# Graph layer on one core: pair products of a message tile in one run, then all its sums, with VectorE's other work behind the pairs

## The reference, cut to what matters

```python
def _L0_gnn_ref(h, V, w_comp, loop_w, bias, ffn_w, ffn_b, ln_g, ln_b, norm, src, dst, etype):
    Hb = jnp.einsum('ni,bio->bno', h, V)
    coef = w_comp[etype]
    m = coef[:, 0][:, None] * Hb[0][src]
    for b in range(1, nb):
        m = m + coef[:, b][:, None] * Hb[b][src]
    m = m * norm[:, None]
    agg = jax.ops.segment_sum(m, dst, num_segments=n_nodes)
    hn = jax.nn.relu(agg + h @ loop_w + bias)
    y = hn @ ffn_w.T + ffn_b + h
    mu = jnp.mean(y, axis=-1, keepdims=True)
    var = jnp.var(y, axis=-1, keepdims=True)
    return (y - mu) / jnp.sqrt(var + EPS) * ln_g + ln_b

x = _layernorm(x + _L0_gnn_ref(x, ..., edge_weight, src, dst, edge_type_8), axis=-1)
x = _layernorm(x + _L1_gnn_ref(x, edge_index, ...), axis=-1)   # two transformer_conv layers
```

## Time and profile before

| | us |
|---|---|
| median of 3 runs | 1980.98 (1979.08 to 1981.27) |
| the profiled execution | 1991.4 |
| its span, first to last instruction | 1989.5 |
| TensorE busy | 1911.6 (96%) |
| VectorE busy | 1450.3 (73%) |
| ScalarE busy | 1282.1 (64%) |
| GpSimd busy | 670.9 (34%) |

### The profile page before, as it was taken

The page is one execution under the profiler, slowest core; times in us unless marked ns, Lnnn a source line. Parts: engine busy times, 40 slices in busy tenths (PEclk is TensorE's granted clock), DMA queues, the critical chain, the costliest instruction groups (busy, mean ns, idle before and its releaser), DMA issues. The chain is left out here.

```text
span 1989.5 us, 53432 instructions
## 1 busy us (share of the span) xinstructions
PE 1911.6 (96%) x19165; PEld 1655.2 (83%) x19165; DVE 1450.3 (73%) x4127; ACT 1282.1 (64%) x2289; POOL 670.9 (34%) x802
## 2 busy tenths in 40 slices
PE   1799999999999999999998999999999999999998
PEld 1789999999999999999995788888887788888887
DVE  3888777878787878787852876666764777777775
ACT  1566767677767766776674666666666566666665
POOL 2576567656765666566500000000000000000000
PEclk9899999999999999999998999999999999999999
DMA  3011111111111111111112222222211332222320
GB/s 82 10 39 54 66 41 40 54 65 40 40 54 65 40 40 53 66 40 41 48 59 100 98 98 97 97 97 97 97 64 46 120 106 96 88 100 99 104 104 11
DMA packets 43018, 137.00 MB, mean 69 GB/s; under 512 B 9190, under 2 KB 24359, under 8 KB 36484
## 3 DMA queue, kind: packets, MB, share of 16 engines
q1 hardware_dynamic: 38484, 128.24, 18.0%
q0 software_dynamic: 4400, 6.80, 1.5%
HBM read 91.83 MB, written 43.20 MB: 68 GB/s over the span
## 5 line engine op out<-in xcount | busy, mean ns | idle before, releaser
L854 PE MATMUL ps<-matrixT,x_rows 125*128 125x256 f32 (+1 forms) x2500 | 563.5, 377 | 0.1
L854 PEld LDWEIGHTS ps<-matrixT,x_rows 125*128 125x128 f32 x2500 | 461.3, 190 | 48.4 <-issue 0.2
L945 ACT COPY matrixT<-ps 125x500 f32<-125x500 f32 (+2 forms) x800 | 382.7, 654 | 54.5 <-PE ps L842 54.1
L1710 DVE CUSTOM_DVE_ANT_0 scores_l<-ps,bias_rows_l 125x500 f32<-125x500 f32 (+1 forms) x700 | 390.0, 619 | 25.7 <-issue 24.9
L842 PE MATMUL ps<-high_weights,low_onehot 64*125 64x125 f32 x6300 | 377.6, 276 | 12.5 <-DVE high_weights L722 11.1
L842 PEld LDWEIGHTS ps<-high_weights,low_onehot 64*125 64x125 f32 x6300 | 362.2, 189 | 31.2 <-issue 17.9
L1611 ACT ACTIVATE scores_l<-scores_l,neg_max_l 125x1500 f32<-125x1500 f32 x200 | 317.3, 1600 | 7.3 <-DVE neg_max_l L1731 7.3
L1499 PEld LDWEIGHTS ps<-weightsT_l,values_l 125*64 125x64 f32 x5000 | 267.9, 136 | 36.4 <-issue 34.1
L1540 PE MATMUL ps<-eye,scores_l 125*125 125x125 f32 x2500 | 295.2, 275 | 0.0
L1540 PEld LDWEIGHTS ps<-eye,scores_l 125*125 125x125 f32 x2500 | 281.2, 189 | 10.1 <-issue 9.6
L1522 PE MATMUL ps<-kT_l,q_tile_l 64*125 64x500 f32 (+1 forms) x1400 | 286.9, 547 | 1.7 <-issue 1.6
(11 more groups left out here) (152 smaller groups left out, 1604.6 us busy)
## 6 DMA issues: line engine op xcount, KB each, us to landing
bias_rows_l<-bias SPq DMA_DIRECT2D x50, 1562.5 KB, 6.6
bias<-bias SPq DMA_DIRECT2D x75, 500.0 KB
x_rows<-in_x SPq DMA_DIRECT2D x1, 1562.5 KB
bias<-bias SPq DMA_DIRECT2D x25, 62.5 KB
x<-x_rows SPq DMA_DIRECT2D x25, 62.5 KB
x_rows_l<-x SPq DMA_DIRECT2D x25, 62.5 KB
out<-rows_l SPq DMA_DIRECT2D x25, 62.5 KB
dst_int<-in_dst SPq DMA_DIRECT2D x1, 402.8 KB
```

Source lines behind the costliest of these rows:

```text
L854: last = nc.tensor.matmul(psG[:, BASES * SPLIT * side:BASES * (SPLIT * side + SIDE[side])], x[:, h, :], MT[side][:, 0:SIDE[side], BASES * ...
L945: last = nc.scalar.copy(MT[side][:, at:at + 2 * c - 1:2, 0:COLS], psP[2 * (g % 3) + q][0:R, :].rearrange("p (i c) -> p i c", c=128)[:, 0:c ...
L1710: V.tensor_tensor_reduce(S[par][:, hd, lo:hi], score_bank(t, HEADS * n + hd)[0:R, 0:cw[j]], bias[par][0:R, lo:hi], 1.0, FLOOR, ALU.add, AL ...
```

## The change

`PARTS` is cut anew (side 0 in three parts, side 1 in five). TensorE multiplies all 63 pairs of tile w, then forms both sides of its sums in the same step, side 0 first; the digits, codes, counts, accumulation and ffn product lie between the parts. ScalarE evacuates both sides in one run, copies both sides of the counts piece by piece behind the logs, and copies the sums out once per tile instead of twice. On VectorE the builds of units 4 to 7 come first in a step; search, second, search_row, third, the bias rows and slot_kinds come behind them, among the builds of the next tile's units 0 to 3. The rings (four units, three pairs of banks, one matrix) keep their sizes, and GpSimd's and SP's programs are as before.

```diff
-PARTS = ((0, 7, 14, 20, T), (0, 9, 18, T))
+PARTS = ((0, 9, 18, T), (0, 5, 10, 15, 20, T))
@@ VectorE, step
                     if k == 0 and inside(z):
                         first(z, 1 - par)
-                    if k == 2 and inside(z):
+                    if k == 4 and inside(t) and (not is_int(t) or t >= EARLY):
+                        search(nc, v, m, t, par)
+                    if k == 4 and inside(z):
                         second(z, 1 - par)
-                    if k == 4 and inside(z):
-                        third(z, 1 - par)
-                    if k == 4 and inside(u):
-                        bias_row(u, 3)
-                    if k == 1 and inside(t) and (not is_int(t) or t >= EARLY):
-                        search(nc, v, m, t, par)
...
-                    if k == 2 and inside(t - 1) and (not is_int(t) or t > EARLY):
+                    if k == 4 and inside(t - 1) and (not is_int(t) or t > EARLY):
                         search_row(t - 1, 1 - par)
+                    if k == 5 and inside(z):
+                        third(z, 1 - par)
                     if k == UNITS - 1 and inside(t - 1) and (not is_int(t) or t > 2):
                         slot_kinds(t - 1, 1 - par)
                     if k < UNITS - AHEAD and inside(w):
                         build_hot(w, 1 - par, k + AHEAD)
                     if k >= UNITS - AHEAD and inside(w + 1):
                         build_hot(w + 1, par, k + AHEAD - UNITS)
-                    if k == 2 and inside(u):
+                    if k == 5 and inside(u):
                         bias_row(u, 0)
-                    if k == 3 and inside(u):
+                    if k == 6 and inside(u):
                         bias_row(u, 1)
+                    if k == UNITS - 1 and inside(u):
                         bias_row(u, 2)
+                        bias_row(u, 3)
@@ TensorE, sums
-                if hi == T:
+                if side == 1 and hi == T:
                     last.then_inc(agg_ok, 1)
@@ TensorE, step
                 if inside(w):
                     pair_products(w, 0)
+                    pair_products(w, 1)
                 if inside(z):
                     pe.wait_ge(y_ok, z + 1)
-                if inside(u):
-                    for i in range(3):
-                        if i > 0:
-                            read(u, i - 1)
-                        turn_counts(u, i)
-                        sums(u, 1, i)
-                    read(u, 2)
-                    turn_counts(u, 3)
                 if inside(w + 1):
                     turn_digits(w + 1, par)
-                if inside(u):
-                    sums(u, 1, 3)
+                if inside(w):
+                    sums(w, 0, 0)
                 if inside(w + 1):
-                    read(u, 3)
                     pe.wait_ge(digitsT_ok, w + 2)
                     turn_codes(w + 1, par)
                 if inside(w):
-                    if w > 0:
-                        pair_products(w, 1)
-                    sums(w, 0, 0)
+                    sums(w, 0, 1)
...
+                if inside(u):
+                    turn_counts(u, 0)
+                if inside(w):
+                    sums(w, 0, 2)
+                for i in range(1, PIECES):
+                    if inside(u):
+                        read(u, i - 1)
+                        turn_counts(u, i)
+                    if inside(w):
+                        sums(w, 1, i - 1)
...
                     last.then_inc(m_ps, 1)
                 if inside(w):
-                    sums(w, 0, 1)
+                    sums(w, 1, 3)
...
                     nc.tensor.matmul(psY, hT[:, :], ffnT[:, :], start=True, stop=True).then_inc(y_ps, 1)
                 if inside(w):
-                    sums(w, 0, 2)
+                    sums(w, 1, 4)
@@ ScalarE, step
                 if inside(u):
-                    sums_out(u, 0)
+                    sums_out(u)
                 if inside(w):
                     evacuate(w, 0)
-                if inside(u):
-                    logs(u, 0)
...
+                    evacuate(w, 1)
                 if inside(w + 1):
...
-                if inside(w):
-                    if not is_int(w) or w > 0:
-                        evacuate(w, 1)
-                    for piece in range(PIECES):
-                        counts_out(w, 0, piece)
...
+                for i in range(PIECES):
+                    if inside(u):
+                        logs(u, i)
+                        if i == 0:
+                            nc.scalar.copy(xt[:, :], xT[:, bass.ds(u * R, R)]).then_inc(xt_ok, 1)
+                    if inside(w):
+                        counts_out(w, 0, i)
+                        counts_out(w, 1, i)
```

More of the change, by code:

```diff
@@ L846, in sums @@
             def sums(s, side, part):
-                lo, hi = PARTS[1 - side][part:part + 2]
+                lo, hi = PARTS[side][part:part + 2]
                 if part == 0:
                     pe.wait_ge(evac_ok, s * FOURS + UNITS * (side + 1))
-                    if side or s >= 1:
-                        pe.wait_ge(aggT_ok, s * 2 + side)
+                    if side == 0 and s >= 1:
+                        pe.wait_ge(aggT_ok, s)
                 for h in range(lo, hi):
@@ L907, in step @@
                     turn_ffn(nc, pe, m, turned_ps, psM)
+                if u == 0:
+                    pe.wait_ge(turned_ok, len(TURNS) + 1)
+                if inside(u):
[8 more added lines that the diff above has]
+                        sums(w, 1, i - 1)
                 if inside(z):
@@ L938, in evacuate @@
                 if not is_int(w) or w >= 1:
-                    act.wait_ge(agg_ok, w * 2 - 1 + side)
+                    act.wait_ge(agg_ok, w)
                     act.wait_ge((ctA_ok, ctB_ok)[side], w * PIECES)
@@ L957, in counts_out, with sums_out @@
                                    (ctA_ok, ctB_ok)[side], 1)
-            def sums_out(s, side):
-                act.wait_ge(agg_ok, s * 2 + side + 1)
+            def sums_out(s):
+                act.wait_ge(agg_ok, s + 1)
                 if not is_int(s) or s >= 1:
                     act.wait_ge(m_ps, s)
-                lo, n = SPLIT * side, SIDE[side]
-                nc.scalar.copy(aggT[:, :, lo:lo + n],
-                               psG[:, BASES * lo:BASES * (lo + n)].rearrange("p (n b) -> p b n", b=BASES)).then_inc(aggT_ok, 1)
+                nc.scalar.copy(aggT[:, :, :], psG[:, 0:BASES * R].rearrange("p (n b) -> p b n", b=BASES)).then_inc(aggT_ok, 1)
             def logs(u, i):
@@ L977, in step @@
                 if inside(u):
-                    sums_out(u, 0)
+                    sums_out(u)
                 if inside(w):
                     evacuate(w, 0)
-                if inside(u):
-                    logs(u, 0)
-                    nc.scalar.copy(xt[:, :], xT[:, bass.ds(u * R, R)]).then_inc(xt_ok, 1)
-                    logs(u, 1)
-                    logs(u, 2)
+                    evacuate(w, 1)
                 if inside(w + 1):
@@ L993, in step @@
                     last.then_inc(digitsT_ok, 1)
-                if inside(u):
-                    logs(u, 3)
-                    sums_out(u, 1)
-                if is_int(w) and w == 0:
-                    evacuate(w, 1)
-                if inside(w + 1):
                     act.wait_ge(codes_ps, w + 2)
@@ L1024, in step @@
                     nc.scalar.copy(xT[:, bass.ds(z * R, R)], psX).then_inc(x_t_ok, 1)
-                if inside(w):
-                    for piece in range(PIECES):
-                        counts_out(w, 1, piece)
             pipeline_loop(act, step, AFTER, LEAD)
```

7 lines of the change are left out of this document (1 added, 6 removed).

## The result

The kernel after takes 2030.9 us (median of 4 runs, 2020.7 to 2039.6) against 1980.2 us (1979.1 to 1981.3) for the kernel before beside it: a ratio of 1.0255, 95% interval 1.0233 to 1.0276, or +50.7 us. Its profiled execution took 2029.3 us, with a span of 2027.3.

The account below looks back on a forecast made before the run. TensorE, busy 96% of the span, was taken as the bound; 22 periods at +2.1 us gave 46 us, start and end 0: 2037 profiled, 2027 against the median, 2031 with a dearer last build; entered 2029, range 1990 to 2070.

Parts of the forecast that it names:

- VectorE's builds set the run: Pair run: units 4 to 7 must be built during it; unit 7 ready at 15.3 to 15.6 us, wanted 12.9.
- Where GpSimd's products lie: Counted from E, the pair run's end: products start 7.5 us before the next run, reach 9.8 to 12 us into it.
- The price of a build: VectorE's four builds inside the run: three dear at 3.7 us beside GpSimd's products, the last quiet at 2.1 to 2.4.
- The run: TensorE's single pair run per tile: about 17.1 us instead of 14.78; less 0.3 for the switch, +2.1 us per tile.
- ScalarE's pace: ScalarE's copies in the pair run: if they alone paced it, 14.6 us, the same as the two runs' 14.78.
- rival 1: GpSimd doesn't collide with the builds; ScalarE's copies pace the run: 8 us faster, 1973 us; chance 0.10.
- the switch: TensorE, one switch from pairs to sums and back removed per tile: saves 0.3 us, between 0 and 0.5.
- Start and end: Message stage's ends: tile 2 starts 5 to 8 us later, the end takes 6 to 7 us less; entered 0.
- The other moved work at no cost: Bias rows, logs, stores and gathers moved: logs have about 2 us slack, stores hold nobody up, late gathers a cost.
- rival 3: TensorE's clock falls after its new waits: 1.7 us per tile, 2066 us if in all tiles; chance 0.13.

Follow-up runs that it names:

- e1: Kernel after with two of GpSimd's four rounds of coefficient products per tile left out: 1982.1 us, ratio 1.0005 to the kernel before.
- e7: Kernel before, unchanged, profiled a second time: 1981.7 us, span 1979.7.
- e6: Kernel after with slot_kinds and GpSimd's coefficient products one pipeline step later, beside the sums: 2018.1 us, ratio 1.0193 to the kernel before.
- e2: Kernel after with a fifth round of GpSimd's coefficient products per tile: 2063.1 us, ratio 1.0418 to the kernel before.
- e5: Kernel after with VectorE's search, second, search_row and third put back among the builds of the run: 2126.0 us, ratio 1.0735 to the kernel before.
- e3: Kernel after with search, second and search_row ahead of the builds on VectorE: 2067.0 us, ratio 1.0433 to the kernel before.
- e4: As e3, with slot_kinds two units earlier so that GpSimd's products start sooner: 2091.6 us, ratio 1.0555 to the kernel before.

## Why the prediction was right, and where it was not

It said 2029 us, 1990 to 2070, with 0.86 on slower. The time is 2030.9.

- *VectorE's builds set the run*: right. The waits are those of L842 for L722; e1 takes the collision away and the loss with it.
- *Where GpSimd's products lie*: right. They were to start 7.5 us ahead of the run and reach 9.8, more like 12 us into it; it is 7.3 and 10.6. slot_kinds starts 31.3 us into the period, which is E + 14.9.
- *The price of a build*: 3.7, 3.7, 3.7 and 2.1 to 2.4 us were expected, 3.67, 3.95, 2.81 and 2.03 came. The second is dearer than the rows the forecast went by, but the third was mis-sized: it lies beside the products for under 1 us, because they end at 10.6 and not at 12. So unit 7 is ready at 14.5 instead of 15.3 to 15.6, and only units 5 and 6 keep TensorE waiting, 1.4 us in all; unit 7 comes just as TensorE is done with 6. The exclusive lock of the rule cited there (the Trainium skill, "SBUF — State Buffer", section "SBUF: two separate sides") agrees with all three instructions of a build being longer in company (L719 2.05 us against 1.19, L722 1.51 against 0.98) and GpSimd's too (L577 up to 1.3 against 0.46). The consequence drawn there, that every build in company pays the upper price, does not hold: one took 2.56 us in tile 14. No run here tells a lock from another way of sharing.
- *Slips in the working*: 17.1 less 14.78 is 2.3 and not 2.4, so the term by its own numbers was 2.0 and not 2.1; and the build from 541.09 to 543.92 took 2.83 us, not 2.9. Neither moves the forecast by more than 2 us.
- *The run*: 17.1 us expected, 16.66 in the mean, 16.38 in most tiles. The term was to be +2.1 us per tile. Against the profile that I worked from it is +1.75, so 38.6 us and not 46; against e7's it is +2.2. Here two errors offset: the runs after were shorter than I had it, and so were the runs before, whose second took 7.0 us in e7 and not 7.57. I took the 10.4 us between profile and median as a constant of profiling; it was a property of that execution, and it sat in this very term. The forecast is closer than its working deserves.
- *ScalarE's pace*: 14.6 us for a run that nothing else disturbs; 14.68 to 14.75 in e1 and e6. But rival 1's gain of 8 us does not exist: e1 is at 1.0005. With the two runs at 14.23 us (e7) instead of 14.78, there was nothing to win; the switch saves 0.2 us of the rest (24.9 against 25.1), the longer run at ScalarE's pace takes back 0.45.
- *Start and end*: +5 to 8 and -6 to -7 expected, +2.8 and -4.4 measured; the sum, entered as 0, is -1.6.
- *The other moved work at no cost*: right for the logs and the stores, no idle time in the rest. The gathers were named as a cost if they land late, with no number. Five times between 200 and 1000 us slot_kinds waits for the last gather, 1.4 to 4.3 us; behind the longer of these waits the products go on until about 16 to 17.4 us into the next run, and periods of 42.2 to 43.8 stand among those of 41.25 (tiles 5, 7, 9 and 14). All this adds about 7 us to the profile. That it also makes the spread of the runs, 2021 to 2040, is likely, since the kernel before spreads over 2 us, but not shown.
- *The clock* (rival 3): did not come. Waits of 0.61 and 0.80 us leave the granted clock at 1.00, and so do the 1.32 and 1.69 us of e2, though the prediction's pattern for it was 1.27 and 1.99 us. It did come in e5 with 1.01 and 3.19 us in every tile, and in some tiles of e3 and e4 with single waits of some 2.1 and 2.2 us. The Trainium skill tells of kernels whose clock falls in every iteration ("TensorE: Matmul & The Clock Gate", section "HAM oscillation — how this bites in real kernels"); e5 is one, the kernel after is not.

No version tried beats the kernel before. A ring of more units, which would let VectorE make more of the run ahead, was not tried.

## What to carry to other kernels

Before merging two bursts that a ring feeds, count how many units the producer must now make inside the burst, and price them by rows in which its neighbour is at work, not by the quiet ones. An engine with 34% busy time over the span is not harmless (in this stage GpSimd is at 63%): where its instructions lie beside the producer's decides, and moving them moves the loss, as e4 and e6 show. Before taking the difference between a profile and a median as a constant, look for the term of the sum in which it sits.

## What was not expected of the hardware

- A build takes 2.29 us alone and up to 3.95 us beside GpSimd's products, 72% more; GpSimd's smallest product goes from 0.46 to up to 1.3 us in VectorE's company. Both engines lose, and which of them loses more changes from one build to the next (2.56 us in tile 14, with GpSimd's root at 1.61 us instead of 0.57).
- The signal of one of TensorE's first three groups reaches ScalarE 0.5 us late, and up to 2.5 us, beside stores on some occasions (or chips), and on time on others; the kernel before stands at 1980 or at 1991 us accordingly.
- Two idle times of 1.01 and 3.19 us per 46 us come before a fall of the clock in every tile of e5 from 2 to 23, a single one of some 2.1 us (longer in one tile) in ten of 22 tiles of e3. Two of 1.32 and 1.69 us per 43 us in e2 do not bring it down, nor 0.61 and 0.80 us per 41 us in the kernel after.
